# Decoder layer on one core: the next step's values behind product 6, their copies and sums behind products 5 and 7

## The reference, cut to what matters

```python
x = x + attention(layernorm(x))                 # latent attention, 32 heads, 2048 16 batches of 128 tokens, causal
x = x + cross_attention(layernorm(x), ctx_4096)
x = x + ffn(layernorm(x))                       # three dense layers with weights of +1 and -1
# inside attention, per head h and batch b:
scores  = q_lat[h] @ c_kv.T + q_rope[h] @ k_rope.T      # scaled by 1/sqrt(192), causal mask
probs   = softmax(scores)
out_lat = probs @ c_kv                                   # "values" in the kernel
out     = (out_lat @ wuv[h].T) @ w_out[h]                # summed over the heads
```

## Time and profile before

| | |
|---|---|
| runs | 1904.31, 1905.45, 1905.55 us; median 1905.45 |
| profiled execution | 1904.51 us, of which the span of core 0 is 1902.7 us |
| granted TensorE clock | 1.000 over the span |
| busy in the span | PE 1895.1, PEld 1596.3, DVE 1548.5, ACT 1184.2, POOL 1038.3 us |
| a step of a later quad | 9.26 us, or 13.34 us with rope products (steps 1 and 4) |

### The profile page before, as it was taken

The page is one execution under the profiler, slowest core; times in us unless marked ns, Lnnn a source line. Parts: engine busy times, 40 slices in busy tenths (PEclk is TensorE's granted clock), DMA queues, the critical chain, the costliest instruction groups (busy, mean ns, idle before and its releaser), DMA issues.

```text
span 1902.7 us, 32230 instructions
## 1 busy us (share of the span) xinstructions
PE 1895.1 (100%) x9920; PEld 1596.3 (84%) x9920; DVE 1548.5 (81%) x3168; ACT 1184.2 (62%) x2904; POOL 1038.3 (55%) x1019
## 2 busy tenths in 40 slices
PE   9999999999999999999999999999999999999999
PEld 7888888888888888888888888888888877888887
DVE  6778888888888888887888778887878889996677
ACT  5457767676758575765565555655656668766441
POOL 5458777787869696965555556555665511000000
PEclk9999999999999999999999999999999999999999
DMA  9839575657474756698747374474738476466645
GB/s 361 331 113 317 136 256 137 248 134 257 130 269 136 237 166 206 196 322 304 206 154 228 87 232 134 158 206 144 221 87 299 134 257 240 199 221 251 231 149 177
DMA packets 328154, 393.27 MB, mean 207 GB/s; under 512 B 271616, under 2 KB 272384, under 8 KB 313088
## 3 DMA queue, kind: packets, MB, share of 16 engines
q1 hardware_dynamic: 328064, 392.21, 63.5%
HBM read 236.46 MB, written 155.71 MB: 206 GB/s over the span
## 4 chain that ended last, share of the span: by engine, by line
PE 96%; DVE 3%; POOL 1%; issue 0%; ACT 0%; DVEq 0%; ACTq 0%; POOLq 0%
PE at_out L1325 11%; PE at_out L1329 10%; PE at_out L1326 10%; PE at_qbank L55 7%; PE at_qbank L57 7%; PE at_qbank L56 7%; PE at_qbank L1649 3%; PE at_score L1286 3%; PE at_score L1649 3%; PE at_score L1289 3%; PE at_turned L1300 2%; PE at_out L1649 2%; PE at_value L55 2%; PE at_value L56 2%; PE at_value L57 2%; PE at_value L1649 2%
## 5 line engine op out<-in xcount | busy, mean ns | idle before, releaser
L2686 DVE TENSOR_TENSOR at_acc<-at_out,at_acc 128x512 f32<-128x512 f32 x640 | 438.8, 689 | 126.8 <-PE at_out L1329 119.5
L2315 POOL TENSOR_TENSOR at_acc<-at_stage,at_acc 128x512 f32<-128x512 f32 x256 | 331.7, 1296 | 174.5 <-ACT at_stage L1791 164.9
L1325 PE MATMUL at_out<-at_wvo,at_val_hi 128*128 128x512 f32 x896 | 365.5, 408 | 1.0 <-ACT at_stage L1791 0.5
L1329 PE MATMUL at_out<-at_wvo,at_val_lo 128*128 128x512 f32 x896 | 351.4, 392 | 0.0
L1326 PE MATMUL at_out<-at_wvo,at_val_hi 128*128 128x512 f32 x896 | 350.0, 391 | 0.0
L1791 ACT ACTIVATE at_stage<-at_out 128x512 f32<-128x512 f32 x256 | 153.3, 599 | 94.4 <-PE at_out L1329 82.2
L1329 PEld LDWEIGHTS at_out<-at_wvo,at_val_lo 128*128 128x128 f32 x896 | 168.1, 188 | 38.6
L1325 PEld LDWEIGHTS at_out<-at_wvo,at_val_hi 128*128 128x128 f32 x896 | 168.7, 188 | 31.8 <-DVE at_acc L2686 5.3
L1326 PEld LDWEIGHTS at_out<-at_wvo,at_val_hi 128*128 128x128 f32 x896 | 169.1, 189 | 25.4
L1832 ACT ACTIVATE at_pT<-at_turned 128x256 fp32r<-128x256 f32 x128 | 49.0, 383 | 226.8 <-PE at_turned L1300 225.9
L1827 ACT ACTIVATE at_probs<-at_probs,at_row_stats 128x128 f32<-128x128 f32 (+1 forms) x512 | 184.0, 361 | 8.9 <-DVE at_row_stats L2633 8.9
(11 more groups left out here) (323 smaller groups left out, 5041.8 us busy)
## 6 DMA issues: line engine op xcount, KB each, us to landing
parts_d<-at_rope_tmp SPq DMA_DIRECT2D x32, 1024.0 KB, 6.9
at_qrope<-parts_d SPq DMA_DIRECT2D x128, 256.0 KB, 4.6
wvo_d<-at_wvo SPq DMA_DIRECT2D x16, 2048.0 KB, 7.5
at_wvo<-wvo_d SPq DMA_DIRECT2D x16, 2048.0 KB, 8.3
ff_w_d<-ff_w SPq DMA_DIRECT2D x21, 1024.0 KB, 6.4
ff_w<-ff_w_d SPq DMA_DIRECT2D x21, 1024.0 KB, 4.8
ab_raw<-in_w_heads SPq DMA_DIRECT2D x32, 576.0 KB, 6.1
wvo_d<-at_wvo SPq DMA_DIRECT2D x16, 1024.0 KB, 10.2
```

What stands on the lines that cost most here:

```text
L1325: pe.matmul(out, hi, weight[:, 0], start=start, stop=False, skip_group_check=True)
L1329: pe.matmul(out, lo, weight[:, 0], start=False, stop=True, skip_group_check=True).then_inc(out_ready, 1)
L2315: pool.tensor_tensor(at, stage[group][z][:], at, ALU.add).then_inc(pool_added, 1)
L2686: dve.tensor_tensor(at, outb[FACTORS[name][2]][:], at, ALU.add).then_inc(added, 1)
```

## The change

A function `values_sooner` keeps the old order for step 0 of quad 0, for the steps in which combined weights are made (1 and 7 of full quads, 1 of the switch quad) and for the last quad. In the other 104 steps:

- PE: the first slice of the latent query goes ahead of P6, and the values of step s+1 behind P6.
- ACT: the exponentials of s+2 go ahead of the values' copies (`direct_values`).
- DVE: the adds of P5 and P7 (and the reciprocals) go ahead of the values' sums and of `direct_values`, which now stand between the add of P7 and that of P3; the sums come first of the two.

```diff
+        def values_sooner(m, s, kind):
+            return making(kind, s) is not None or opens(m, s) or kind == "last"
...  (PE)
-                if s + 1 < end:
+                if s + 1 < end and values_sooner(m, s, kind):
                     values(m, s + 1, group_of(kind, s + 1))
...
+                next_latent(m, s, end, kind, first, range(1))
                 product_6(m, s, kind)
-                next_latent(m, s, end, kind, first, range(QT - 1))
+                if s + 1 < end and not values_sooner(m, s, kind):
+                    values(m, s + 1, group_of(kind, s + 1))
+                next_latent(m, s, end, kind, first, range(1, QT - 1))
...  (ACT)
-                if s + 1 < end:
+                if s + 1 < end and values_sooner(m, s, kind):
                     direct_values(m, s + 1)
...
                 if s + 2 < end:
                     exps(m, s + 2)
+                if s + 1 < end and not values_sooner(m, s, kind):
+                    direct_values(m, s + 1)
...  (DVE)
-                if s + 1 < end and not opens(m, s, 1):
+                sooner = values_sooner(m, s, kind)
+                if s + 1 < end and sooner and not opens(m, s, 1):
                     direct_values(m, s + 1)
...
-                if s + 1 < end and not late:
+                if s + 1 < end and not late and sooner:
                     value_sums(m, s + 1)
...
                     if not of and not opens(m, s):
                         add_product(m, s, group, "P7", 1, 1)
+                    if s + 1 < end and not sooner:
+                        value_sums(m, s + 1)
+                        direct_values(m, s + 1)
                     add_product(m, s, group, "P3", 0, 1)
```

## The result

The changed kernel takes 1973.35 us, median of four runs (1972.72 to 1973.81), against 1905.43 (1904.31 to 1905.55): the ratio is 1.0358 with a 95% interval of 1.0346 to 1.037. It is slower by 68 us; the forecast was slower by 33, and the time lies 17 us above the range. The profiled span is 1970.9 us against 1902.7.

What follows compares the result with a forecast made beforehand. PE was taken as the bound, busy 1895.1 of 1902.7 us. Losses of 2.98 x 8 = 23.8 us (switch and later quads) and 1.3 x 7 = 9.1 (full quads), together 32.9, gave 1938.5 us; range 1920 to 1956.

Steps and rivals of the forecast that it cites:

- Rivals 1 and 2: 1: time stays, the rests' slack suffices, 1905.5, chance 0.05; 2: faster, fewer stops at values and adds, about 1899, chance 0.05.
- rival 3: Only DVE's add of P4 behind the latent counts in steps 2 and 5, rests free: 22 us, 1927; chance 0.07.
- rival 4: DVE becomes the bound, each of 104 steps loses 0.6 us more: 62 us, 1968; chance 0.07.
- the signs of being wrong: Later quads' steps all 9.26 us, hi copy before +6.5, loss spread evenly, or full quads losing more than later ones.
- PE's own order … I take 0: PE's moved slice and values: P6 at about +2.2, P5 at +4.29, no new waits, loss 0.
- Full quads … steps 0, 2 and 5 have weight products on PE behind P4 …: 0: Quads 0 to 6: weight products or an earlier latent copy leave these steps no loss; 1.3 us a quad in all.
- 0.1 in step 3: Full quads: the rests' load comes at 463.8 instead of 463.64, through the later latent copy; loss 0.1 us.
- the 0.2 forecast for step 4: Full quads: weight copies push DVE's turn about 0.8 us late, costing 0.2 us at P5.
- the sum of a switch or later quad: Quads 7 to 14: late latent copy costs 0.70 and 0.10 (step 2), 0.38 (3), 1.42 (5), 0.38 (7); 2.98 us a quad.
- lateness less 0.11: Price of a PE stop, from one earlier row: a load 0.21 us late lost 0.10 us.
- the 0.10 at P5 of step 3: Switch and later quads: DVE runs 0.7 us late, the add of P6 ends about 0.1 after P5 wants it; 0.10 us.
- the prediction's reading of that rule: Loads pulled ahead would make each stop up to 0.19 us cheaper, some 8 us over about 40 stops; not used.

Runs made afterwards that it cites:

- e6: Changed kernel with the latent slice behind P6 in old-order steps, ACT's latent copy before the sums' hi copy, and full step 6 in the old order: 1903.35 us.
- e1: Changed kernel with the latent query's first slice put back behind P6 in the steps that keep the old order: 1954.02 us, ratio 1.0256.
- e2: Changed kernel with ACT's latent copy ahead of the sums' hi copy and the rope copies in the 104 steps: 1930.00 us, ratio 1.0131.
- e7: Changed kernel with ACT's latent copy ahead of the sums' hi copy in switch and later quads only, not in full quads: 1945.71 us, ratio 1.0211.
- e5: Kernel before with only the latent query's first slice moved ahead of P6, in every step: 1979.19 us, ratio 1.0387.

## Why the prediction was wrong

**Right.** The mechanism it rested on, place by place: the hi copy at +7.65, the latent copy's end at +9.81 with rope copies, the count 0.04 to 0.05 behind the forecast, the 24 stops at the rests, P2's load at +10.70 (forecast +10.61), the steps 1, 4 and 6 of later quads unchanged, and the 1.0 us that DVE carries from full step 6 into step 7 (e6: 7.0 us). The gain was put at 5 us at most and is 0.02 us a step, some 2 us. Rivals 1 and 2 fell, rival 3 by the 20.8 us at the rests, and rival 4, DVE as the bound, since the steps without a named stop are not longer. Of the signs of being wrong one came: the full quads lost more than the later ones, 5.3 us each against 3.3.

**Wrong, the step "PE's own order … I take 0".** "The latent slice ahead of P6 and the values behind it leave P6 at about +2.2" holds where both move. In the steps that keep the old order the values stay, so P6 comes a slice later: the slice waits for the bank of the weights, and P5 for the add of P6. The prediction priced nothing in those steps but DVE's lateness. Cost: 19.3 us (e1).

**Wrong, the step "Full quads … steps 0, 2 and 5 have weight products on PE behind P4 …: 0", and 0.1 in step 3.** These products were taken as cover; those of steps 2 and 3 themselves ask for the latent's bank. Step 2 lost 0.66 us and step 3 1.65; the 0.2 forecast for step 4 did not come. Cost: 15.7 us (e2 against e7). The question "who waits for `q_taken`?" was answered with the rests, though the code of `absorb_pair` asks for the same count.

**Mis-sized, the sum of a switch or later quad.** It was 2.98 us by forecast, 3.4 measured; over eight quads 23.8 against 27.6 (e7). The loss was taken as lateness less 0.11 at every stop, from the earlier trace rows. It consists of two parts: lateness less the lead that the load has over its matmul, and 0.10 us more at the next spacing. Before a 512-column product the lead is 0.23, which gives less 0.11 or so; before the rests it was 0.10 (before, load at 981.74, matmul at 981.84), so a load 0.53 late cost 0.55. There are three such stops a quad. Against it, the 0.10 at P5 of step 3 did not come. The prediction's last sum is off by 0.2 besides: 1937.4 and 0.9 make 1938.3 and not 1938.5.

The tensor engine's pull-ahead of weight loads, for which the prediction names the Trainium skill's page "TensorE: Matmul & The Clock Gate" (Part 2), did not soften the stops shown: the load of the rests starts at 1062.22, 0.10 behind the end of the latent copy in that step, and the first matmul is recorded with it:

```profile
1061.54 0.58 ACT L1819 ACTIVATE at_qlat<-at_qbank 128x512 f32<-128x512 f32 x1
```

```profile
1062.22 0.71 PE L1290 MATMUL at_score<-at_keys,at_qlat 128*128 128x128 f32 x4 [1.32 <-DVEq L2597]
```

By the prediction's reading of that rule the later quads would have lost less than forecast; they lost more.

What is put together: 19.3 (slice) + 15.7 (L1216) + 27.6 (later quads) + 7.0 (full step 7) = 69.6, less about 2 for the shorter steps, is 67.6 of the 67.9 us.

## What to carry to other kernels

List an edit's places from the diff's conditions, not from its description: of two moves that balance each other, check each step in which only one of them is made. When a counted semaphore will come late, search the code for every wait on it, and look first at the work that you mean to take as cover. Two products in one bank need room for the add between them: here 1.7 us from the first matmul of the one to the load of the next, where six matmuls make 1.36 us and nine 2.04. The slice moved out of that gap has 0.68 us of matmuls, and a later step grew by 0.55 (e5).

## What was not expected of the hardware

The price of a stop is not the length of the wait. It is the lateness of the weight load, less the lead that the load had over its matmul, and 0.10 us more in the next spacing. Behind the stop at 1029.88 that spacing is 0.33 us (the next matmul is recorded at 1030.21) where it is 0.227 in a stream, and the four 128-column matmuls from 1062.22 on take 0.55 us to the next group (1062.77) where the four from 981.84 on took 0.45 in the kernel before (982.29). The lead was 0.23 us ahead of 512-column matmuls and 0.10 ahead of the narrow ones, so a late load cost 0.13 less than its lateness in the one place and all of it in the other. The 0.10 us is not peculiar to a stop: P1, whose load has a lead of 0.02 us behind the narrow matmuls, shows the same long spacing in every step in which it waits for nobody (0.55 us over two spacings).

A reader that waits for a count saw it 0.10 us (1062.12 to 1062.22) and 0.11 us (482.24 to 482.35) after the end of the copy behind which it is counted.
